# Edge MLP of a graph kernel: one ScalarE operation for two first layers, other places for three copies, one table instead of two

## What is computed

```
src_f = node_features[src]
dst_f = node_features[dst]
edge_in = concatenate([src_f, dst_f, edge_features], axis=1)   # 128 + 128 + 64
h  = relu(edge_in @ We1 + be1)                                 # 32
edge_msg = relu(h @ We2 + be2)                                 # 128
h2 = relu(concatenate([dst_f, edge_msg], axis=1) @ Wn1 + bn1)  # 64
node_msg = relu(h2 @ Wn2 + bn2)                                # 128
agg = segment_sum(node_msg, dst)
x3 = x2 + node_features + agg
```

## Time and profile before

| | |
|---|---|
| runs without a profile | 3445.94 us (3441.49 to 3449.65) |
| profiled execution | 3449.56 us, of which the span of the trace is 3447.8 us |
| busy over the span | PE 66%, DVE 62%, ACT 49%, POOL 45% |
| granted TensorE clock, mean | 0.786 |
| DMA | 696.61 MB, 202 GB/s |
| attention stage, MLP stage, gather stage | 776, 784, 685 us |

### The profile page before, as it was taken

How to read it: one execution, slowest core, us unless ns; L and a number is a source line. 1 busy time by engine, 2 the same in 40 slices (tenths; PEclk the granted TensorE clock), 3 DMA queues, 4 the chain that set the end, 5 groups by cost and what they waited for, 6 DMA issues and landing times. The chain is left out here.

```text
span 3447.8 us, 49059 instructions
## 1 busy us (share of the span) xinstructions
PE 2259.9 (66%) x10561; PEld 1583.6 (46%) x10561; DVE 2135.4 (62%) x8721; ACT 1690.1 (49%) x4589; POOL 1563.5 (45%) x1491
## 2 busy tenths in 40 slices
PE   4773446377667777777438788888556666664666
PEld 2333414255446666666313343343355555653555
DVE  5797333188757878778657777777343333331899
ACT  2590102188735555555448888888433333331222
POOL 3202673400076767666264656555145565665000
PEclk9896668699866666666759999999867776776899
DMA  2596324399977777766448999989534443441898
GB/s 74 177 378 202 59 65 111 48 314 323 309 222 217 226 215 232 220 213 217 100 144 259 283 277 282 286 273 260 175 123 145 137 147 135 151 141 39 297 318 289
DMA packets 494679, 696.61 MB, mean 202 GB/s; under 512 B 66363, under 2 KB 357398, under 8 KB 485932
## 3 DMA queue, kind: packets, MB, share of 16 engines
q1 hardware_dynamic: 416414, 511.30, 46.5%
q0 software_dynamic: 63360, 130.75, 14.3%
q10 hardware_dynamic: 14736, 52.96, 4.2%
HBM read 394.91 MB, written 327.18 MB: 209 GB/s over the span
## 5 line engine op out<-in xcount | busy, mean ns | idle before, releaser
L274 POOL DMA_INDIRECT xs<-x_d,table_src x400 | 384.5, 961 | 524.4 <-DVE x L1502 154.7
L274 POOL DMA_INDIRECT xs<-n_d,srcI x200 | 213.8, 1069 | 427.1 <-DVEq L1151 270.0
L250 DVE RECIPROCAL rs<-root 128x4 f32<-128x4 f32 (+3 forms) x253 | 52.4, 207 | 528.8 <-ACT root L269 349.2
L1839 PE MATMUL bank<-xs,same 128*128 128x129 f32 x400 | 117.7, 387 | 239.5 <-issue 135.2
L1808 ACT ACTIVATE sums<-bank 128x129 f32<-128x129 f32 x200 | 55.9, 279 | 408.6 <-DMA r_d<-nx 211.2
L274 POOL DMA_INDIRECT xd<-x_d,table_dst x200 | 215.2, 1076 | 65.1 <-issue 65.1
L1716 POOL DMA_INDIRECT r_d<-rd,out_row x200 | 197.5, 988 | 92.8 <-issue 60.3
L274 POOL DMA_INDIRECT xd<-n_d,dstI x200 | 208.2, 1041 | 62.6 <-issue 61.1
L1839 PEld LDWEIGHTS bank<-xs,same 128*128 128x128 f32 x400 | 85.0, 264 | 258.7 <-issue 144.8
L1321 PE MATMUL bank<-xs,same 128*128 128x129 f32 x400 | 127.4, 414 | 102.1 <-ACT sums L1264 53.4
L1657 PEld LDWEIGHTS bank<-nmsg,same 128*128 128x128 f32 x400 | 63.1, 199 | 273.8 <-issue 147.7
(11 more groups left out here) (382 smaller groups left out, 7399.9 us busy)
## 6 DMA issues: line engine op xcount, KB each, us to landing
n_d<-T SPq DMA_DIRECT2D x98, 528.0 KB
nt<-n_d SPq DMA_DIRECT2D x49, 1056.0 KB
r<-r_d SPq DMA_DIRECT2D x98, 520.0 KB, 5.3
bc<-dst_d SPq DMA_DIRECT2D x170, 256.0 KB
r_d<-nv SPq DMA_DIRECT2D x49, 528.0 KB
v_d<-nv SPq DMA_DIRECT2D x49, 528.0 KB
nv<-v_d SPq DMA_DIRECT2D x49, 528.0 KB
x_d<-x SPq DMA_DIRECT2D x100, 256.0 KB
```

Source lines behind the costliest of these rows:

```text
L274: pool.indirect_dma_start(out=out, out_offset=None, in_=table, in_offset=bass.IndirectOffsetOnAxis(ap=index, axis=0)).then_inc(s, 16)
L1839: nc.tensor.matmul(sum_p[:, 0:D + 1], same[:, s % 4, j, :], xs[:, s, j, 0:D + 1], start=True, stop=False)
```

## The change

Four edits are made at once.

1. The first layers of edges (`hidden`, 32 rows) and nodes (`nhidden`, 64 rows) share one PSUM bank: `hidden` of group g writes rows 64 to 95 and, by weights that are zero, zeros to rows 0 to 63; `nhidden` of group g - 1 is added to rows 0 to 63. One ScalarE operation of 96 rows then applies bias and ReLU to both. `hidden` on ScalarE waits for both products. The order of parts on TensorE changes so that `hidden` comes first and `nhidden` after it, with the transposes before `nmessage`.
2. `hsT_copy` and `hdT_copy` copy what was transposed in the same step (lag 3) and stand late in their step instead of first.
3. VectorE takes 4 node tiles instead of 3 (`BD`), ScalarE 4 instead of 5.
4. `x3_d` is gone. x3 is written to `r_d` alone. The gather stage reads whole rows of `r_d` (1040 bytes instead of 512) and writes the normalised rows to a tile `h` of their own. As columns 128 to 259 of the edge rows of `r_d` would otherwise be read unwritten, the attention stage stores zeros there: 512 pieces of 528 bytes in each of 50 steps.

Small additions: four memsets at the start of the MLP stage and one at the start of the attention stage.

```
+        def clear_v(g, s):
+            sp.dma_start(r_d[bass.ds(g * (G * P) + NN, G * P), D:RW].rearrange("(j p) f -> p j f", p=P),
+                         clear[:, :, :]).then_inc(cleared, 16)
...
-        pipeline(sp, NGE, [(bc_used, 4), (load_bc, 0), (load_nodes, 0, -1), (first_used, 6), (load_first, 2), (store, 8),
+        pipeline(sp, NGE, [(bc_used, 4), (load_bc, 0), (load_nodes, 0, -1), (first_used, 6), (load_first, 2), (clear_v, 2), (store, 8),
+        sp.wait_ge(cleared, 16 * NGE)
...
-B, BD, late = 2 * G, 3, 1
+B, BD, late = 2 * G, 4, 1
...
-hid = sb("hid", [32, 2, G * P], F32, c)
-nhid = sb("nhid", [65, 2, G * P], F32, c)
+hid = sb("hid", [97, 2, G * P], F32, c)
...
-hs_p, hd_p, hid_p, msg_p, nhid_p, nmsg_p, sum_p = bank[0], bank[1], bank[2], bank[3], bank[4], bank[5], bank[6]
+hs_p, hd_p, hid_p, msg_p, nmsg_p, sum_p = bank[0], bank[1], [bank[2], bank[4]], bank[3], bank[5], bank[6]
...
         def store(g, s):
             sp.wait_ge(x3_ready, g + 1)
-            sp.dma_start(rows_of(x3_d, g, D, NN), x3[:, s % 4, :, :]).then_inc(stored[s % 4], 16)
+            sp.dma_start(rows_of(r_d, g, D, NN), x3[:, s % 4, :, :]).then_inc(stored[s % 4], 16)
...
         def store_x3(g, s):
             sp.wait_ge(nx_ready, g + 1)
-            sp.dma_start(chunk_of(x3_d, g, 0, D), nx[:, s % 4, :, :]).then_inc(nx_stored[s % 4], 16)
             sp.dma_start(chunk_of(r_d, g, 0, D), nx[:, s % 4, :, :]).then_inc(nx_stored[s % 4], 16)
...
-        nc.vector.memset(nhid[64:65, :, :], 1.0)
+        nc.vector.memset(hid[96:97, :, :], 1.0)
+        for n in ("We1a", "We1b", "We1c"):
+            nc.vector.memset(W[n][:, 0:64], 0.0)
+        nc.vector.memset(W["Wn2"][64:96, :], 0.0)
...
-        pipeline(dve, NGE, [(inverse, 2), (hdT_copy, 4), (weigh, 2 + late, -1), (own, 7), (weighed, 2 + late, -1),
+        pipeline(dve, NGE, [(inverse, 2), (weigh, 2 + late, -1), (own, 7), (weighed, 2 + late, -1),
-                            (differences, 1), (sames, 5), (squares, 1), (total, 1)], S8)
+                            (differences, 1), (sames, 5), (squares, 1), (total, 1), (hdT_copy, 3)], S8)
...
         def hidden(g, s):
-            act.wait_ge(hid_ps, g + 1)
-            nc.scalar.activation(hid[:, s % 2, :], hid_p[0:32, :], ACT.Relu, bias=C["be1"][0:32, :]).then_inc(hid_in, 1)
+            if isinstance(g, int) and g == NGE:
+                act.wait_ge(nhid_ps, NGE)
+                rows = slice(0, 64)
+            else:
+                act.wait_ge(hid_ps, g + 1)
+                if not (isinstance(g, int) and g == 0):
+                    act.wait_ge(nhid_ps, g)
+                rows = slice(0, 96)
+            nc.scalar.activation(hid[rows, s % 2, :], hid_p[s % 2][rows, :], ACT.Relu, bias=C["b1"][rows, :]).then_inc(hid_in, 1)
...
-        def nhidden(g, s):
-            act.wait_ge(nhid_ps, g + 1)
-            nc.scalar.activation(nhid[0:64, s % 2, :], nhid_p[0:64, :], ACT.Relu, bias=C["bn1"][0:64, :]).then_inc(nhid_in, 1)
...
-        pipeline(act, NGE, [(hsT_copy, 4), (total(0), 6), (nodes_h2, 2, -1), (nhidden, 5), (total(1), 6), (hidden, 4),
-                            (total(2), 6), (relus, 2), (nmessage, 5), (message, 4), (total(3), 6), (nodes_v, 2 + late, -1),
+        pipeline(act, NGE, [(total(0), 6), (nodes_h2, 2, -1), (total(1), 6), (hidden, 4, 1), (total(2), 6),
+                            (relus, 2), (nmessage, 5), (hsT_copy, 3), (message, 4), (total(3), 6), (nodes_v, 2 + late, -1),
...
             last.then_inc(hT_ps, 1)
 
         def hidden(g, s):
+            out = hid_p[s % 2][0:96, :]
             pe.wait_ge(hsT_in, g + 1)
-            nc.tensor.matmul(hid_p[0:32, :], W["We1a"][:, 0:32], hsT[:, s % 2, :], start=True, stop=False)
+            nc.tensor.matmul(out, W["We1a"][:, 0:96], hsT[:, s % 2, :], start=True, stop=False, skip_group_check=True)
             pe.wait_ge(hdT_in, g + 1)
-            nc.tensor.matmul(hid_p[0:32, :], W["We1b"][:, 0:32], hdT[:, s % 2, :], start=False, stop=False)
+            nc.tensor.matmul(out, W["We1b"][:, 0:96], hdT[:, s % 2, :], start=False, stop=False, skip_group_check=True)
             hold("pe", pe, ef_in[s % 4], count4(g, s))
-            nc.tensor.matmul(hid_p[0:32, :], W["We1c"][0:64, 0:32], efT[:, s % 4, :], start=False,
-                             stop=True).then_inc(hid_ps, 1)
+            nc.tensor.matmul(out, W["We1c"][0:64, 0:96], efT[:, s % 4, :], start=False, stop=False,
+                             skip_group_check=True).then_inc(hid_ps, 1)
 
         def message(g, s):
             pe.wait_ge(hid_in, g + 1)
-            nc.tensor.matmul(msg_p[:, :], W["We2"][0:32, :], hid[:, s % 2, :], start=True, stop=True).then_inc(msg_ps, 1)
+            nc.tensor.matmul(msg_p[:, :], W["We2"][64:96, :], hid[64:96, s % 2, :], start=True, stop=True).then_inc(msg_ps, 1)
 
         def nhidden(g, s):
-            nc.tensor.matmul(nhid_p[0:64, :], W["Wn1a"][:, 0:64], hdT[:, s % 2, :], start=True, stop=False)
+            alone = isinstance(g, int) and g == NGE - 1
+            out = hid_p[(s + 1) % 2][0:64, :]
+            nc.tensor.matmul(out, W["Wn1a"][:, 0:64], hdT[:, s % 2, :], start=alone, stop=False, skip_group_check=True)
             pe.wait_ge(msg_in, g + 1)
-            nc.tensor.matmul(nhid_p[0:64, :], W["Wn1b"][:, 0:64], msg[:, s % 2, :], start=False,
-                             stop=True).then_inc(nhid_ps, 1)
+            nc.tensor.matmul(out, W["Wn1b"][:, 0:64], msg[:, s % 2, :], start=False, stop=True,
+                             skip_group_check=True).then_inc(nhid_ps, 1)
 
         def nmessage(g, s):
-            pe.wait_ge(nhid_in, g + 1)
-            for j in range(G):
-                last = nc.tensor.matmul(nmsg_p[:, j * P:(j + 1) * P], nhid[:, s % 2, j * P:(j + 1) * P],
-                                        W["Wn2"][0:65, :], start=True, stop=True)
+            pe.wait_ge(hid_in, g + 2)
+            for j in range(G):
+                last = nc.tensor.matmul(nmsg_p[:, j * P:(j + 1) * P], hid[0:97, (s + 1) % 2, j * P:(j + 1) * P],
+                                        W["Wn2"][0:97, :], start=True, stop=True)
             last.then_inc(nmsg_ps, 1)
 
         def total(j):
...
-        pipeline(pe, NGE, [(total(0), 6), (nhidden, 5), (total(1), 6), (hidden, 4), (total(2), 6),
-                           (nmessage, 5), (message, 4), (total(3), 6), (transposes, 3)], S8)
+        pipeline(pe, NGE, [(total(0), 6), (hidden, 4), (total(1), 6), (nhidden, 5), (total(2), 6),
+                           (transposes, 3), (nmessage, 5), (total(3), 6), (message, 4)], S8)
-xs = sb("xs", [P, S8, G, TW], F32, c)
+xs = sb("xs", [P, S8, G, RW], F32, c)
+h = sb("h", [P, 4, G, TW], F32, c)
...
-                gather(pool, xs[:, s, j, 0:D], x3_d, table_src[:, edges:edges + 1], src_in[s])
+                gather(pool, xs[:, s, j, :], r_d, table_src[:, edges:edges + 1], src_in[s])
...
-            sp.dma_start(rd[:, s, :, 0:D], rows_of(x3_d, g, D, NN)).then_inc(dst_in[s], 16)
+            sp.dma_start(rd[:, s, :, 0:D], rows_of(r_d, g, D, NN)).then_inc(dst_in[s], 16)
...
-                nc.scalar.activation(xs[:, s, j, 0:D], xs[:, s, j, 0:D], ACT.Relu, bias=nb[:, s, j:j + 1],
+                nc.scalar.activation(h[:, s % 4, j, 0:D], xs[:, s, j, 0:D], ACT.Relu, bias=nb[:, s, j:j + 1],
```

31 lines of the change are left out of this document (17 added, 14 removed).

## The result

The changed kernel took 3477.62 us (median of 4 runs, 3463.0 to 3484.1) beside 3443.72 us of the kernel before on the same chip (4 runs): a ratio of 1.0116, interval 1.0072 to 1.0161. The forecast was 3400. The profiled execution took 3463.0 us, with a span of 3461.2 and a mean granted clock of 0.778; it is the fastest of the four, so the two profiles differ by only 13.4 us of the medians' 34.

What follows compares the result with a forecast made beforehand. ScalarE's own order in the MLP stage, with two short trips to other engines, was taken as the bound. 3449.6 - 50 + 3 = 3402.6, with the median 3.6 lower: forecast 3400 us, range 3372 to 3440.

Steps and rivals of the forecast that it cites:

- That is a tie, and I cost it at nothing: MLP stage: ScalarE's wait for nhidden ahead of hidden, product ready 0.1 us before it is asked for, cost nothing.
- the whole gain of 50: MLP stage: 49 steps with nodes, each 1.03 us shorter, make 50 us.
- The count: MLP stage, from ScalarE's last total: nhidden ready at 6.43 us, ScalarE there at 6.53.
- a rival with a chance of 0.13: MLP stage: slow clock falls on hidden and nhidden, loses 1.0 us a step, result 3449; chance 0.13.
- the clock would rise: TensorE, MLP stage: moving the transposes shortens the quiet stretch before the slow products, so PEclk goes above 0.92.
- 1.03 us a step: MLP stage: 0.57 for the nhid operation, 0.39 for a node tile, 0.07 for the copies; 13.75 becomes 12.72.
- Ahead of the node tiles: ScalarE, MLP stage: wait of about 1.0 us a step; root to first node tile goes from 2.02 to 1.48.
- The third total: ScalarE, MLP stage: the wait ahead of it stays at 0.75 us a step, bounds 0 and 1.02.
- the 0.07 for the two copies: MLP stage: hdT leaving the way to the offset saves 0.54, hsT in the open costs 0.47; together 0.07 a step.
- The third rival: Attention and gather stages: wide-table transfers lengthen steps by their whole time, 42 + 51 us, result 3490; chance 0.12.
- The zeros: Attention stage: storing them adds 0.27 MB a step, taken as 1 us in all, bounds 0 and 42.
- The second rival: MLP stage: with a steady clock the third total comes in time, 37 us more gained, result 3363; chance 0.1.

Runs made afterwards that it cites:

- the fill: Changed kernel plus two unread products at the end of TensorE's step in the MLP stage: 0.9888, 0.9861 and 0.9937 of the kernel before.
- group 1: Follow-up runs sharing one chip, on which the kernel before took 3169.3 us; the changed kernel was run there only with two unread products, at 3141.22 us.
- the run before it: Kernel before plus two unread products at the end of TensorE's step in the MLP stage: 3171.79 us, 0.9997.
- the table alone: Kernel before with only the single wide table, its stored zeros and the gathers of 1040 bytes: 3488.76 us, 0.9982.
- without the table: Changed kernel with both tables and the narrow gathers of the kernel before: 3513.47 us, 1.0033 of the kernel before.
- group 2: Follow-up runs sharing one chip, on which the kernel before took 3498.8 us; its unchanged repeat took 3495.08 us, 0.9986.
- group 3: Follow-up runs sharing one chip, on which the kernel before took 3503.4 us and the changed kernel 3496.46 us, 0.9968.

## Why the prediction was wrong

**The step that failed** is the sentence "That is a tie, and I cost it at nothing", with the ground given for it, the granted clock of 1.00. In the profile of after this wait is 1.32 us a step, 65 us over 49 steps, more than the whole gain of 50. The count itself was right: in the 5 steps of 43 that ran at the full clock the products were ready at 6.34 us (forecast 6.43), ScalarE came at 6.64 (6.53) and waited 0.00. In the other 38 the products were ready at 7.97 and ScalarE waited 1.46. So the condition of the tie held in one step of nine. The 0.49 to 0.54 that are left with the fill come from the fill, which delays the first total, and not from the tie.

**The clock.** I used a clock of 1.00 for the chain, though the earlier trace rows showed half-speed products in the very next step, and left the other case to a rival with a chance of 0.13. Its mechanism is what happened: the lower level moved from `nhidden` to `hidden`. Its size, at most the gain, was too small, since I held the share of slow time at today's 0.08 of clock and it doubled to 0.15. I had argued from the gap before the first total alone; the gap ahead of the second total, which the long `hidden` now covers, was in none of my rows, and with it gone the same idleness makes longer gaps. Whether that is why the clock fell isn't shown: a filled gap raised it from 0.83 to 0.97, but the kernel before kept 0.91 with 15 long gaps, and edit 2 alone had 0.91 beside 0.95 without longer ones.

The Trainium skill (TensorE: Matmul & The Clock Gate, Part 4: PE-mode transpose) says that a transpose doesn't count as a busy TensorE in the way that a product does. I drew from it that the clock would rise, as the transposes left the place before the gap. It fell from 0.92 to 0.85, and with edit 2 alone it was 0.91 beside 0.95. What I drew from the rule is wrong for this kernel; the rule itself is not tested, for no run moves the transposes alone.

**The work removed.** 1.03 us a step fits: the step of after is 12.72 and the waits, within 0.05. In group 1 the step went from 13.51 to 12.82, by 0.69, with the 0.54 ahead of `hid` in it. But neither edit 2 nor edit 3 brings its term alone (+12 us and 0 in the stage), and with the clock up the stage was 28 us shorter than the variants of the kernel before, not 50. A removed operation pays only until the next wait: with edit 3, `hid` took 0.47 us a step more idle time than in the run before it.

**Ahead of the node tiles** 1.12 us a step (forecast about 1.0); root to the first node tile is 1.59 in the step shown (1.48). **The third total** was misread: the 0.83 (0.75) is the wait of all four totals. By the operation before them in the timeline, the third has 18.9 / 42 = 0.45 (before, 27.3 us of the 32.5, 0.63), and 12.0 / 42 = 0.29 stand ahead of the second, behind the node tiles, where the kernel before had next to none; the forecast has no such wait. The two errors nearly cancel, and that is luck. That the 0.07 for the two copies holds inside the whole change isn't shown; edit 2 alone costs. **VectorE** idles 143.8 us ahead of its reciprocal, 3.4 a step instead of 2; the step is 1.57 longer than forecast, which is the difference.

**The third rival** (the wide table is paid for) is refuted. The gather stage is 680.8 beside 681.0 us, the gathers of 1040 bytes take what those of 512 took, and VectorE still waits for ScalarE's root there:

```profile
L273 POOL DMA_INDIRECT xs<-r_d,table_src x200 | 194.1, 970 | 268.0 <-PE bank L1867 90.0
```

```profile
L249 DVE RECIPROCAL rs<-root 128x8 f32<-128x8 f32 x39 | 7.9, 203 | 306.1 <-ACT root L268 254.3 <-issue 51.7
```

The Trainium skill (DMA: Bandwidth & Descriptors, How a descriptor splits into AXI transactions) would make pieces at a pitch of 1040 bytes dearer; if they are, it is hidden here, with the DMA engines at 0.50. **The zeros** of the attention stage cost nothing either: 756.0 beside 771.5 us, and 787.0 beside 796.5 with the table alone. Why attention is 15 us shorter in after is open. No edit aims at it, the changed kernel's attention took 756.0, 800.9 and 770.8 us in its three profiles, and without this the result would have been farther from the forecast.

**The second rival** (the third total in time) is seen only in group 1, where all totals wait 0.28 us in the changed kernel with the fill, 0.23 in the kernel before with it and 0.01 with edit 3. So it belongs to the group, not to the change.

**The range.** Its lower end, 3372, doesn't follow from its words: a third of the second rival's 37 us and no cost elsewhere make 3400 - 12 - 3 = 3385. The result lies beyond the other end.

What stays open: the size of the loss in the whole time. The MLP stage was longer than before wherever the two can be compared (+31.4 on the first chip, +22.5 and, without the table, +11.1 in group 2; the 805.7 of group 3 have no profile of the kernel before beside them), but the ratio was 1.0116 on the first chip and 0.9968 in group 3.
